# A conditioned transformer block on one core: VectorE transposes the probabilities of fifteen groups of sixteen, ScalarE applies the whole FiLM of the tokens, and the squares go behind the exponentials

## What is computed

```python
h = film(rmsnorm(x, norm1_w), cond, film1_w, film1_b)
Q, K, V = h @ q_w + q_b, h @ k_w + k_b, h @ v_w + v_b
attn = softmax(einsum('bnd,bmd->bnm', Q, K) * D ** (-0.5))
x = x + (einsum('bnm,bmd->bnd', attn, V) @ proj_w + proj_b)
h = film(rmsnorm(x, norm2_w), cond, film2_w, film2_b)
out = x + gelu(h @ mlp_w1 + mlp_b1) @ mlp_w2 + mlp_b2
```

## Time and profile before

| | us |
|---|---|
| three timed runs | 1741.82, 1738.18, 2941.28 |
| their median | 1741.82 |
| the profiled execution | 1739.0 |
| its span | 1737.2 |

### The profile page before, as it was taken

The page is one execution under the profiler, slowest core; times in us unless marked ns, Lnnn a source line. Parts: engine busy times, 40 slices in busy tenths (PEclk is TensorE's granted clock), DMA queues, the critical chain, the costliest instruction groups (busy, mean ns, idle before and its releaser), DMA issues.

```text
span 1737.2 us, 23173 instructions
## 1 busy us (share of the span) xinstructions
PE 1732.7 (100%) x8210; PEld 1455.3 (84%) x8210; DVE 1325.3 (76%) x1891; ACT 892.0 (51%) x1497; POOL 197.7 (11%) x204
## 2 busy tenths in 40 slices
PE   9999999999999999999999999999999999999999
PEld 8888888888888888888888888888888888888887
DVE  6878778888876886697688769768866975885477
ACT  6545454664644654554465455446544554653344
POOL 1567676000000000000000000000000000000000
PEclk9999999999999999999999999999999999999999
DMA  9487787633247678677767867876877777677676
GB/s 359 136 281 282 264 299 278 255 128 90 57 173 205 192 266 266 205 241 265 231 189 265 269 206 237 266 233 193 267 265 206 231 264 240 191 242 246 194 221 210
DMA packets 201858, 395.56 MB, mean 228 GB/s; under 512 B 23888, under 2 KB 27984, under 8 KB 199696
## 3 DMA queue, kind: packets, MB, share of 16 engines
q1 hardware_dynamic: 201488, 393.55, 69.2%
q0 software_dynamic: 112, 0.26, 0.0%
q10 hardware_dynamic: 144, 0.26, 0.0%
HBM read 330.99 MB, written 62.98 MB: 227 GB/s over the span
## 4 chain that ended last, share of the span: by engine, by line
PE 96%; POOL 1%; DVE 1%; DMA 1%; ACT 0%; issue 0%; SPq 0%; POOLq 0%
PE psum L750 35%; PE psum L770 23%; PE psum L606 12%; PE psum L778 12%; PE psum L720 3%; PE psum L655 2%; PE psum L656 2%; PE psum L660 2%; PE psum L629 1%; DMA f2w_sb<-f2w_dram 1%; PE psum L671 1%; PE psum L675 1%; PE psum L670 1%; POOL w_out L570 1%; PE psum L818 0%; PE psum L640 0%
## 5 line engine op out<-in xcount | busy, mean ns | idle before, releaser
L750 PE MATMUL psum<-op_hi_P,ring 128*128 128x512 f32 x1792 | 552.0, 389 | 0.0
L770 PE MATMUL psum<-stage_hi,ring 128*128 128x512 f32 x1784 | 440.6, 389 | 0.0
L750 PEld LDWEIGHTS psum<-op_hi_P,ring 128*128 128x128 f32 x1792 | 336.3, 188 | 69.7
L770 PEld LDWEIGHTS psum<-stage_hi,ring 128*128 128x128 f32 x1784 | 334.9, 188 | 69.5
L1002 ACT CAST stage_hi<-x 128x1024 fp32r<-128x1024 f32 x224 | 235.3, 1054 | 235.2 <-PE psum L770 223.1
L750 PE MATMUL psum<-op_lo_P,ring 128*128 128x512 f32 x896 | 348.6, 389 | 0.0
L1470 DVE TENSOR_TENSOR stage_lo<-x,stage_hi 128x1024 fp32r<-128x1024 f32 x224 | 273.3, 1223 | 72.4 <-ACT stage_hi L1002 72.2
L986 ACT ACTIVATE x<-x,vecs 128x512 f32<-128x512 f32 x192 | 138.1, 723 | 278.2 <-DVE x L1457 278.2
L778 PE MATMUL psum<-stage_lo,ring 128*128 128x512 f32 x892 | 238.4, 389 | 0.0
L750 PEld LDWEIGHTS psum<-op_lo_P,ring 128*128 128x128 f32 x896 | 168.2, 188 | 34.8
L778 PEld LDWEIGHTS psum<-stage_lo,ring 128*128 128x128 f32 x892 | 167.5, 188 | 34.7
(11 more groups left out here) (194 smaller groups left out, 2309.4 us busy)
## 6 DMA issues: line engine op xcount, KB each, us to landing
ring<-wu_scratch SPq DMA_DIRECT2D x448, 256.0 KB, 2.9
ring<-wd_scratch SPq DMA_DIRECT2D x448, 256.0 KB, 2.9
x_tok<-x_dram SPq DMA_DIRECT2D x16, 1024.0 KB, 11.4
xT_in<-xT_dram SPq DMA_DIRECT2D x16, 1024.0 KB, 8.9
x2T_scratch<-xT_in SPq DMA_DIRECT2D x32, 512.0 KB, 4.4
hn<-x2T_scratch SPq DMA_DIRECT2D x32, 512.0 KB, 5.3
xres<-x2T_scratch SPq DMA_DIRECT2D x32, 512.0 KB, 5.5
out_dram<-xres SPq DMA_DIRECT2D x31, 512.0 KB, 4.3
```

The costliest lines, as they stand in the source:

```text
L750: mm = pe.matmul(to, wt, b, start=q in FRESH and t == 0, stop=t == len(steps) - 1, skip_group_check=True)
L770: mm = pe.matmul(bank(q, dt), a[:, dt, part, :], stage_hi[r][:, e, :], start=q in FRESH and ss == 0 and e == 0 and part == 0, stop=False, ...
```

## The change

`BY_BLOCKS` goes from 8 to 0: VectorE's 16 block transposes, and with them `g_pair`, the early `h_high` and the early `h_lo`, now serve the groups 0 to 14, and TensorE transposes only those of group 15. VectorE's `modulate` is gone from the loop (it stays for group 0, ahead of the loop). ScalarE does all four blocks, the first two between its copies of the third and the fourth quarter of `g`. `sum_squares` and `modulate_pair` go behind the exponentials. The four `film2_high` of group 9 stand together behind `keep_g(9, 3)`. One warm-up matmul goes.

```diff
-WARM_UP = 10
-BY_BLOCKS = 8
+WARM_UP = 9
+BY_BLOCKS = 0
...
             def h_high(m, k):
-                if k < 2:
-                    act.wait_ge(h_done_dve, 2 * m + k + 1)
+                if m == 0 and k < 2:
+                    act.wait_ge(h_done_dve, k + 1)
                 else:
-                    act.wait_ge(h_done_act, 2 * m + k - 1)
+                    act.wait_ge(h_done_act, KD * m + k - 1)
...
-                if n == 9:
-                    act.wait_ge(loaded["f2w"], 16)
-                    for r in range(WOUT):
-                        act.wait_ge(w_stored[r], 16 * (7 * CHUNKS // WOUT))
-                    film2_high(0)
-                    film2_high(1)
+                if n < LAST:
+                    wait_used(act, scored, n)
+                    modulate(n + 1, 0)
+                    modulate(n + 1, 1)
                 if n > 0:
                     keep_g(n, 3)
...
+                if n == 9:
+                    act.wait_ge(loaded["f2w"], 16)
+                    for r in range(WOUT):
+                        act.wait_ge(w_stored[r], 16 * (7 * CHUNKS // WOUT))
+                    for k in range(KD):
+                        film2_high(k)
                 if n < LAST:
-                    wait_used(act, scored, n)
                     modulate(n + 1, 2)
                     modulate(n + 1, 3)
...
-                if n in (13, 14):
-                    modulate_pair(0, 2 * (n - 13))
-                if 0 < n <= LAST - 3 and n != 9:
-                    sum_squares(n + 3)
...
-                if n == 9:
-                    film2_high(2)
-                    film2_high(3)
...
+                if 0 < n <= LAST - 3:
                     sum_squares(n + 3)
+                if n in (13, 14):
+                    modulate_pair(0, 2 * (n - 13))
...
             def key_terms(n):
...
-                dve.wait_ge(h_done_act, 2 * n + 2)
-                dve.wait_ge(h_done_dve, 2 * n + 2)
+                dve.wait_ge(h_done_act, KD * n + 2)
+                if n == 0:
+                    dve.wait_ge(h_done_dve, 2)
...
                     scale_x(n + 1)
-                    modulate(n + 1, 0)
-                    modulate(n + 1, 1)
```

## The result

The changed kernel takes 1755.05 us (median of 6 runs, 1753.36 to 1756.17), the kernel before 1740.99; the ratio is 1.0085, with a 95% interval of 1.0075 to 1.0096. The forecast was 1751, within 2%.

The account below looks back on a forecast made before the run. TensorE, busy 1732.7 of 1737.2 us, was taken to bound the kernel. Matmuls and warm-up removed -3.8 - 0.2, waits +13.1 + 1.5 + 1.5, sum +12.1 on 1739.0: 1751 us, range 1734 to 1762.

Parts of the forecast that it names:

- The loop: From one group's scores to the next one's, through VectorE and ScalarE: 30.8 us against the 29.16 TensorE needs.
- The choice between the ends: Loop length taken as 30.8 us, nearer the 30.4 sum of measured terms than the upper end of 32.0.
- The eight waits: TensorE waits 1.6 us at the scores of each of groups 1 to 8, 13.1 us in all.
- The gain of 0.47 us a group: Eight groups without transposing matmuls fall from 29.63 to 29.16 us, taking 3.8 us off TensorE.
- Group 0: TensorE waits once, 1.5 us (0 to 2), for group 0's block transposes after `g_pair`.
- Group 9: TensorE waits 1.5 us (0 to 4) at the product of the second FiLM, whose weights come later.
- The second half of the attention gains nothing and loses nothing: From group 8 on GpSimd is idle and the loop is at most 27.6 us, so time is unchanged.
- Gain stands: Rival: `h_lo` in groups 1 to 8 hardly slowed, under 4.0 us, loop below 29.16; 1737 us; chance 0.2.
- The transposes are slowed too: Rival: GpSimd holds up VectorE's block transposes, about 1.5 us more a group, 12 in all; 1763 us; chance 0.1.
- Only the weights are late: Rival: loop hidden, TensorE waits only in group 9 for later weights, some 5 us; 1741.5 us; chance 0.1.

Follow-up runs that it names:

- gpsimd_no_reads: The changed kernel with GpSimd's sums and splits of the MLP weights replaced by constants, so it reads nothing; 1739.6 us, ratio 0.9995.
- after_early: The changed kernel with GpSimd's chunk let go at the division and the next weights' load behind the third split; 1744.07 us, ratio 1.003.
- film_behind_g: The changed kernel with ScalarE's first two FiLM blocks moved behind its copy of the last quarter of g; 1743.38 us, ratio 1.0017.
- after_early_g11: after_early with the first two FiLM blocks behind the fourth copy of g in group 11 alone; 1742.45 us, ratio 1.0019.
- early_load: film_behind_g with the row of sums copied ahead of the squares in group 11 and the weights' load behind the third split; 1739.3 us, ratio 1.0001.
- early_chunk: early_load with GpSimd's chunk let go at the division, ahead of the block transposes; 1736.81 us, ratio 0.9986.
- film_only: The changed kernel with BY_BLOCKS back at 8, so TensorE transposes in groups 0 to 7 again; 1743.48 us, ratio 1.0018.
- before_early: The kernel before with GpSimd's chunk let go at the division and the next weights' load behind the third split; 1749.6 us, ratio 1.0052.
- transposes_only: The kernel before with BY_BLOCKS at 0 and nothing else, so VectorE transposes and keeps its FiLM; 1770.51 us, ratio 1.0173.

## Why the prediction was right, step by step

- *The loop.* Forecast 30.8 us, measured 30.9. Its terms in the changed profile, forecast in brackets: maximum to bias 2.12 (2.55), `h_lo` 4.34 (5.33), division 1.81 (0.7), transposes 5.09 (5.08), key terms 3.66 (3.67), residual and key split 4.42 (3.77), first `scale_x` 1.77 (1.33), FiLM and `g` 3.77 (3.98), scores 3.84 (3.73), handing over 0.1 (0.3). They add up to 30.9. What decided, that `h_lo` and its neighbours now fall into GpSimd's chunk, is shown by gpsimd_no_reads and after_early. No run frees `h_lo` alone. By the rows the loop holds some 5.6 us of hold-up (an estimate): `h_lo` 1.9, the bias 1.1, the division 0.9, the key split 0.9 and the first `scale_x` 0.7; without `h_lo`'s share it would be 29.0, just under TensorE's 29.16. The single sizes missed both ways: `h_lo` is slowed 1.8 times, not 2.1, the division is caught whole, and the split pays for the long sums at the chunk's head. The choice between the ends, near the sum of the measured terms, came out through errors that cancel: with `h_lo` at its measured 4.34 and the other ten terms as forecast, the sum would have been 29.45 and the wait 0.3. So the 30.8 was in part luck. One sum was also wrong as written: 27.6 is the loop with `h_lo` alone free; with "the rest free" too it is 26.6 by the same terms. Both lie under 29.16, so nothing hung on it.
- *The eight waits.* Forecast 1.6 us each, measured 1.4 at the scores; the periods are 1.7 us longer than 29.16, since the matmuls around the wait read longer too. The gain of 0.47 us a group was right: the periods of film_behind_g and gpsimd_no_reads are 29.16.
- *Group 0.* Forecast 1.5 us. In the changed kernel's profile the wait is not there, since TensorE itself was late; where it started early (gpsimd_no_reads, after_early, after_early_g11, early_load, early_chunk) it is 1.5 or 1.6.
- *Group 9.* Forecast 1.5 us, measured none. The wait is real in film_behind_g and early_load (3.0 and 2.2), where TensorE gets to group 9 sooner. Two terms were off by a microsecond each, in the same direction: the load was issued 25.0 us behind the start of chunk 7 (289.69 to 314.73), not 26.1, and TensorE came to the product 46.4 us behind that start, not 45.2.
- *"The second half of the attention gains nothing and loses nothing"* is the step that failed. In group 10 VectorE adds up the squares of pair 0, four instructions that take 4.9 us ahead of `scale_x`, and the FiLM behind it now stands ahead of `g`. Timelines of the changed kernel's DVE, then ACT:

```profile
385.04 1.22 DVE L1275 TENSOR_TENSOR sq_attn<-sq_attn 128x1024 f32<-128x1024 f32 x1
...
390.65 2.50 DVE L1203 SCALAR_TENSOR_TENSOR h<-xT_in,norm_row 128x512 f32<-128x512 f32 x4
```

```profile
391.47 3.18 ACT L915 ACTIVATE h<-h,film 128x128 f32<-128x128 f32 x8
394.56 0.67 ACT L943 ACTIVATE g<-psum,wk_bq 128x512 f32<-128x512 f32 x1
```

  That is the 2.54 us at 395.28, 2.7 us of the 16.2, and the one wait of the scores in film_only. I had the loop of the late groups at 27.6 us and did not look for what else stands in it once.
- *The start.* 2.3 us that I had not foreseen, and that need not be the change's. TensorE waited 1.64 us at 25 us for `wp_lo`, since the weights landed later (ScalarE, which waits for them, goes on at 22.68 us; before it was 20.91). Instructions up to there are the same in after_early, which began its first scores at 48.97. Of the eleven experiments' profiles five began them near 51.4 and six near 49.1, some with nine warm-up matmuls and some with ten on the late side. The executions of the kernel before spread by as much: of the 25 beside the first four experiments, 15 took 1738.4 to 1739.8 us and 10 took 1741.2 to 1744.3. The mean granted clock was 1.000 in all of the 15 and 0.999 or less in nine of the 10, as in the profiles that began late, but none of the 25 has a trace to show its start. Of the changed kernel five executions in six had the lower clock, so it isn't excluded that the change makes the late start more frequent.
- *Rivals.* "Gain stands" is wrong: `h_lo` took 4.34 us, over the 4.0 that the prediction set for it, though only by 0.3. "The transposes are slowed too" is wrong: 0.303 us each beside GpSimd's sums. "Only the weights are late" is what film_behind_g turned into, once the loop was away.

## What to carry to other kernels

When work moves onto an engine, write down the closed loop that it now stands in, with each term at its contended duration, and lay the neighbour's busy stretch over it: what decides is which instructions fall into that stretch, and letting the stretch begin at the division, ahead of the transposes and the key terms (8.8 us in the changed kernel's order), was worth some 10 us here, and cost 10 in the kernel before, where another instruction fell into it. Put what releases TensorE ahead of what only prepares the next group, since the same work behind the copy of `g` cost nothing in the groups 1 to 8. And look through the loop for what stands in it in one group only.

## What was unexpected of the hardware

- The block transposes are immune, as the forecast took them to be without a row to show it: 5.04 or 5.05 us for 16, with GpSimd idle or in the middle of its 1.3 us sums. That makes them a good cover for GpSimd's work.
- An instruction of 128 x 4 elements can be held as long as a large one: the bias of the exponentials took 1.27 us in the changed kernel's group 7, 0.16 with GpSimd out of the way.
- Two full-size inputs are not needed to be held up. The first key term has one (L1228 `key_bias<-h`, with two columns of constants): 0.55 us with GpSimd idle, 0.97 in early_chunk and 1.50 in before_early, beside GpSimd's chunk. VectorE's FiLM has one as well, and took 3.82 us in the earlier trace rows and 2.15 in group 9 of the same kernel.
- A wait of one to four microseconds can cost TensorE more than itself. In film_only 32 scores took 5.47 us behind the wait of 2.55 us in group 11, in place of 3.73, and the granted clock from 383 to 393 us was 0.83. It isn't so each time: behind the same wait, 2.54 us, the changed kernel's took 3.84, at a clock of 1.00 from 390 to 400, and group 11 to 12 was 1.6 us shorter (29.75 against 31.36). In transposes_only the clock fell in the periods with waits of 2.33, 3.70, 3.75 and 3.77 us and stayed at 1.00 in those with 1.09 to 2.13. And it fell around the 1.64 us for `wp_lo`. From 20 to 30 us, the changed kernel first, then the one before (window, its length, busy of PE, PEld, DVE, ACT, POOL, granted clock, DMA share, GB/s):

```profile
20.00:30.00 10.00, 8.37 (x46) 7.23 (x46) 6.08 (x11) 6.67 (x17) 0.00 (x0) 0.83 1.05 396
```

```profile
20.00:30.00 10.00, 10.00 (x66) 8.97 (x65) 7.87 (x15) 7.07 (x18) 0.00 (x0) 1.00 1.04 381
```
